# Cross-attention, second pass: eight key tiles of a block taken as 4 and 4 instead of 3, 3 and 2

## The reference

```python
def _L1_xattn_ref(x, latents, Wq, Wkv, Wout, gm, bm, gl, bl):
    ...
    xn = layernorm(x, gm, bm)            # x is the context, 8192 rows
    ln = layernorm(latents, gl, bl)      # 512 rows
    q = ln @ Wq
    kv_input = jnp.concatenate([xn, ln], axis=-2)
    kv = kv_input @ Wkv
    k, v = jnp.split(kv, 2, axis=-1)
    ...
    q, k, v = (heads(q), heads(k), heads(v))   # 8 heads of 64
    q = q / scale
    sim = jnp.einsum('bhid,bhjd->bhij', q, k)
    sim = sim - jax.lax.stop_gradient(jnp.max(sim, axis=-1, keepdims=True))
    attn = jax.nn.softmax(sim, axis=-1)
    out = jnp.einsum('bhij,bhjd->bhid', attn, v)
    ...
    return out @ Wout
```

## Time and profile before

| what | value |
|---|---|
| median of 3 runs | 2656.38 us (2655.33 to 2661.38) |
| the profiled execution | 2653.46 us |
| its span | 2651.8 us |
| mean granted TensorE clock | 0.969 |
| second pass of the cross-attention | about 1335 to 1864 us |
| TensorE busy | 2490.5 us, 94% |
| VectorE busy | 1809.0 us, 68% |
| ScalarE busy | 1122.2 us, 42% |

### The profile page before, as it was taken

How to read it: one execution, slowest core, us unless ns; L and a number is a source line. 1 busy time by engine, 2 the same in 40 slices (tenths; PEclk the granted TensorE clock), 3 DMA queues, 4 the chain that set the end, 5 groups by cost and what they waited for, 6 DMA issues and landing times.

```text
span 2651.8 us, 33253 instructions
## 1 busy us (share of the span) xinstructions
PE 2490.5 (94%) x11614; PEld 1681.0 (63%) x11618; DVE 1809.0 (68%) x1885; ACT 1122.2 (42%) x1366; POOL 592.2 (22%) x404
## 2 busy tenths in 40 slices
PE   6999989988776999999999999999898899999998
PEld 5778877654334777776655555555586777777775
DVE  5878855499988677778976666666445766666665
ACT  2334422466344222222255555555233455455543
POOL 4555544488842211111100000000000000000000
PEclk9999998999877999999999999999898899999999
DMA  7667755722021343343233232232112255666663
GB/s 276 231 237 259 264 153 171 258 72 72 2 101 42 127 169 148 127 182 136 96 124 108 96 96 73 96 108 84 64 64 115 104 219 214 237 229 230 216 218 137
DMA packets 124235, 394.70 MB, mean 149 GB/s; under 512 B 23728, under 2 KB 39292, under 8 KB 97136
## 3 DMA queue, kind: packets, MB, share of 16 engines
q1 hardware_dynamic: 95584, 326.82, 34.8%
q10 hardware_dynamic: 28560, 66.66, 7.2%
HBM read 304.14 MB, written 89.30 MB: 148 GB/s over the span
## 4 chain that ended last, share of the span: by engine, by line
PE 79%; DVE 8%; DMA 5%; POOL 3%; issue 3%; ACT 2%; ACTq 0%; SPq 0%; DVEq 0%; POOLq 0%
PE ps L2109 18%; PE ps L2110 17%; PE ps L2111 17%; PE ps L2496 10%; PE ps L2506 9%; PE ps L2403 3%; DMA w_halves<-unit_lo 3%; DVE ps L1642 2%; POOL work L951 1%; PE ps L2757 1%; DMA wT_lo<-w_halves 1%; DMA sh_raw<-in_s_parts 1%; DMA x_res<-in_x 1%; POOL work L932 1%; DVE ln_st L1512 1%
## 5 line engine op out<-in xcount | busy, mean ns | idle before, releaser
L1862 DVE TENSOR_TENSOR sums<-sums,pT 128x1024 f32<-128x1024 f32 x272 | 319.2, 1222 | 194.0 <-ACT pT L1341 192.9
L1800 DVE SCALAR_TENSOR_TENSOR peak<-ps,rs_all,peak 128x1024 f32<-128x1024 f32 x272 | 335.7, 1279 | 93.9 <-PE ps L2403 93.6
L1341 ACT ACTIVATE pT<-ps,rs_all 128x1024 f32<-128x1024 f32 x272 | 284.8, 1111 | 230.8 <-PE ps L2496 184.9
L2506 PE MATMUL ps<-pT,values 128*64 128x512 f32 x1088 | 256.4, 602 | 0.0
L2226 PE MATMUL ps<-work,ident 128*128 128x512 f32 x256 | 130.3, 641 | 33.6 <-POOL work L932 18.6
L1001 POOL TENSOR_TENSOR cT_lo<-cT_raw,cT_hi 128x512 fp32r<-128x512 f32 x60 | 77.6, 1293 | 352.1 <-ACT cT_hi L1290 352.1
L2506 PEld LDWEIGHTS ps<-pT,values 128*64 128x64 f32 x1088 | 68.8, 136 | 132.9 <-issue 112.0
L1996 DVE TENSOR_TENSOR rgu_lo<-rgu_raw,rgu_hi 128x2048 fp32r<-128x2048 f32 x64 | 143.9, 2289 | 5.1 <-ACT rgu_hi L1424 5.0
L894 POOL TENSOR_TENSOR ctx_lo<-ctx_raw,ctx_hi 128x512 fp32r<-128x512 f32 x64 | 105.2, 1643 | 131.7 <-DVE ctx_hi L1547 131.7
L1642 DVE TENSOR_TENSOR_SCAN ps<-ps,work 128x1024 f32<-128x1024 f32 x50 | 114.3, 2285 | 13.2 <-ACT ps L1213 11.2
L1028 POOL TENSOR_SCALAR ln_ve<-ln_mv 128x1 f32<-128x1 f32 x4 | 1.5, 379 | 537.0 <-DVE ln_mv L1513 537.0
(11 more groups left out here) (470 smaller groups left out, 6429.9 us busy)
## 6 DMA issues: line engine op xcount, KB each, us to landing
rgu_raw<-in_r_gate_up SPq DMA_DIRECT2D x64, 1024.0 KB, 4.8
rd_raw<-in_r_down SPq DMA_DIRECT2D x32, 1024.0 KB, 4.8
sh_raw<-in_s_parts SPq DMA_DIRECT2D x32, 768.0 KB, 4.3
key_rows<-key_hi SPq DMA_DIRECT2D x17, 1024.0 KB, 3.9
key_rows<-key_lo SPq DMA_DIRECT2D x17, 1024.0 KB, 6.0
value_rows<-values SPq DMA_DIRECT2D x17, 1024.0 KB, 8.9
ctxT_raw<-in_ctx_T SPq DMA_DIRECT2D x16, 1024.0 KB, 6.8
ctx_raw<-in_ctx SPq DMA_DIRECT2D x16, 1024.0 KB, 8.5
```

The source lines that it names most:

```text
L1341: nc.scalar.activation(pT[:, i], ps[:, b:b + 2], ACT.Exp, scale=rs_all[:, bass.ds(c * KT + attend_tile(j, i)[1], 1)]).then_inc(s4_exp.sem, 1)
L1800: nc.vector.scalar_tensor_tensor(peak[:, p], ps[:, b:b + 2], rs_all[:, bass.ds(c * KT + kt, 1)], peak[:, p], ALU.mult, ALU.max).then_inc(s ...
L1862: nc.vector.tensor_tensor(sums[:, p], sums[:, p], pT[:, i], ALU.add).then_inc(s4_sum.sem, 1)
L2506: done = nc.tensor.matmul(ps[e * DK:(e + 1) * DK, 6 + p], values[:, s, kt, h * DK:(h + 1) * DK], pT[:, i, e], start=start and kt == 0, sto ...
```

## The change

`attend_groups` gives blocks 2 to 32 two groups, (0, 1, 2, 3) and (4, 5, 6, 7). Blocks 0 and 1 keep four groups of two, and block 33 keeps 3, 3 and 2. The products behind a block's first group are now of tiles 4 to 7 of the block before, except in blocks 1 and 2, whose predecessors end with the group (6, 7). For that reason blocks 2 and 3 are written out on TensorE, and its first loop has 6 turns instead of 7. In block 2, now a plain number, tile 2 waits for the last shift rows and not for an exponential, since its place has not been used before. ScalarE, VectorE and SyncE have the same instructions and waits as before.

```diff
 def attend_groups(j):
 
-    return ((0, 1), (2, 3), (4, 5), (6, 7)) if isinstance(j, int) and j < 2 else ((0, 1, 2), (3, 4, 5), (6, 7))
+    if isinstance(j, int) and j < 2:
+        return ((0, 1), (2, 3), (4, 5), (6, 7))
+    if isinstance(j, int) and j == BLOCKS - 1:
+        return ((0, 1, 2), (3, 4, 5), (6, 7))
+    return ((0, 1, 2, 3), (4, 5, 6, 7))
...
                     else:
                         if isinstance(j, int) and j == 1:
                             shift_transpose(3)
-                        weigh_values(j - 1, 1 - s, 0 if isinstance(j, int) and j == KCHUNKS else half, (6, 7),
-                                     stop=isinstance(j, int) and j == KCHUNKS)
+                        weigh_values(j - 1, 1 - s, 0 if isinstance(j, int) and j == KCHUNKS else half,
+                                     (6, 7) if isinstance(j, int) and j <= 2 else (4, 5, 6, 7), stop=isinstance(j, int) and j == KCHUNKS)
 
             attend_pe(0, 1, 0, 32, start=True)
             attend_pe(1, 0, 0, 32)
-            with pe.Fori(0, LEFT) as q:
-                attend_pe(q * 2 + 2, 1, 0, q * 80 + 112)
-                attend_pe(q * 2 + 3, 0, 0, q * 80 + 112)
+            for j in range(2, 4):
+                attend_pe(j, 1 - j % 2, 0, 112)
+            with pe.Fori(0, LEFT - 1) as q:
+                attend_pe(q * 2 + 4, 1, 0, q * 80 + 192)
+                attend_pe(q * 2 + 5, 0, 0, q * 80 + 192)
```

## The result

The changed kernel takes 2646.95 us (median of 22 runs, 2637.16 to 2651.07), the kernel before 2654.94 in the runs beside it (22 runs, 2641.55 to 2661.38). The ratio is 0.997 with a 95% interval of 0.9961 to 0.998, so 5 to 10 us faster. The profiled execution has a span of 2643.0 us, against 2651.8.

The account below looks back on a forecast made before the run. TensorE's own order of work, busy 94%, was taken as the bound. With the load becoming the limit, 3.4 us from 28 blocks plus 0.7 from three gave 4.1, taken as 4.5: 2656.38 to 2651.9 us, range 2645.5 to 2663.

Parts of the forecast that it names:

- (a): TensorE, blocks 2 to 32: one round trip fewer each, 0.35 us, 10.9 us in all if nothing new waits.
- (b): Fourth tile of a group waits for the first tile's exponential, twice a block; 0 to 0.06 us each, 0.06 taken.
- (c): Next block's load is issued later, at 7.77 us, and becomes the limit: period 15.17 instead of 15.29 us.
- The sign that I had named: Period from one block's first similarities to the next in the changed profile: 15.1 to 15.2 us, not 14.9.
- Full gain (1): Loads land in time and exponentials hold nothing up; 7.1 to 10.9 us gained, 2645.5 to 2649.3 us; chance 0.18.
- The load wait with a loss (2): TensorE waits on `kv_loaded` at the heads of 28 blocks; 5.7 to 25 us slower, 2662 to 2682; chance 0.16.
- Exponentials (3): Fourth tile held 0.25 us instead of 0.06 by its exponential; 4.7 us slower, 2661 us; chance 0.09.
- The loop part (d): Blocks 2 and 3 written out on TensorE, and block 2's other wait for tile 2: no effect.

Follow-up runs that it names:

- keys early: Changed kernel with a block's keys and scale rows issued after the similarities, only values still after the products; 2641.02 us, ratio 0.9949 to before.
- groups of two: Kernel before with groups of two tiles in all blocks, four round trips instead of three; 2666.93 us, ratio 1.0063 to before.
- groups of six: Changed kernel with keys early and groups (0, 1) and (2 to 7); ratio 0.9974 to before, pass 483.08 us.
- The second comparison: The changed kernel run again unaltered, against the kernel before; 2649.7 us, ratio 0.9979.
- the two kernels with the latest loads: Changed kernel with the load held back until tile 4's similarities, ratio 1.0104; changed kernel with scale rows issued ahead of keys and values, ratio 1.0067.

## Why the prediction was right

**The round trip** (a). Predicted 0.35 us each, 31 of them, 10.9 us. Measured with nothing in the way (keys early against before): 489.41 - 478.08 = 11.3 us, 0.37 each; from the other side, groups of two, 0.37 in the mean of all blocks but 17. Right, shown twice. What in a round trip costs the time was not separated. The rows only show where it stands: 0.32 instead of 0.23 us from the last pair of a similarity group to the products, 0.34 instead of 0.23 behind the first pair of a group, and 0.14 behind the products. That the change of the tiles' shape does it, and not for instance the order of the weight loads, is argued and not shown.

**The fourth tile** (b). Predicted up to 0.06 us for each wait. In the changed kernel the exponential, the weight load and the matmul of the fourth tile, and the addition that takes the same result, answer to the earlier trace rows:

```profile
1501.49 4.13 ACT L1345 ACTIVATE pT<-ps,rs_all 128x1024 f32<-128x1024 f32 x4 [3.43 <-PE ps L2500]
...
1502.54 0.42 PE L2500 MATMUL ps<-shift_rows,scale_rows 64*128 64x512 f32 x2
1502.66 0.19 PEld L2500 LDWEIGHTS ps<-q_lo,key_hi 64*128 64x128 f32 x2
1502.73 4.63 DVE L1866 TENSOR_TENSOR sums<-sums,pT 128x1024 f32<-128x1024 f32 x4 [2.93 <-ACT pT L1345]
```

The weight load stands at 1502.66, 0.12 behind the matmul it would have gone with (1502.54), 2.74 us after the group's start, inside the 2.68 to 2.81 that were read from the exponential. Its matmul started at 1502.77, 0.23 after the one before, so unhindered. The wait is real and costs 0, since half of the weight load's lead of 0.23 us took it up. I had taken the upper end, a release at 2.81 and 0.11 from the weight load to the matmul. The weight load came at 2.74, and the groups of six show a matmul 0.03 behind its weight load, so the 0.11 is no least distance either.

**The load** (c). The mechanism is the one predicted: issue, landing, and a block that starts with the later of the two. This is the step that carried the forecast, and its size was somewhat off. Predicted were an issue at 7.77, 6.9 to the last byte, 0.45 to the count and 0.05 to go on: 15.17 us. Measured: 7.71 and 7.32, which is 15.03. So 0.06 too much is from (b), 0.08 from the landing. The saving of a usual block was thus 0.26 to 0.28 us and not 0.12. What made the total less wrong than that were the seven longer blocks, which I had not predicted: they hold the mean at 15.11. The sign that I had named, a period of 15.1 to 15.2 us, fits this mean and not the usual block, and that is luck. Over the pass: 4.5 us predicted, 6.25 and 3.7 measured in two traces.

**The total.** 2651.9 us was predicted against a median of 2656.38; with the runs beside it the median of before is 2654.94 and the change is worth 8.0 us (5.3 to 10.4), which is more than the 4.5 predicted. The second comparison gave 0.9979, 5.6 us. Both are more than the passes of the two traces show, 6.25 and 3.7, but both intervals take these in, so chance may be all of it. What moves the stages outside the pass stays open: two traces of the same changed kernel already differ by 1.3 us at the start of block 2 and by 1.9 behind the pass.

**The rivals.** Full gain (1) needed the loads to land in time; they do not, but with keys early it is what one gets. The load wait with a loss (2) was the right wait at a price that did not come about: its point was put at 7.47 us from issue to landing, and it is 7.3; only single blocks passed it, as block 19 with 16.08 us. The rule of the Trainium skill that the prediction names (DMA: Bandwidth & Descriptors, Anatomy of one DMA), by which most of 2 us lies between the last byte and the semaphore, is stated there for transfers issued by GpSimd; these are issued by SyncE. It is not borne out here: from last bytes at 1514.50 to TensorE's start at 1514.95 is 0.45 us. Exponentials (3) cost nothing at four and five tiles, and 0.16 us a block at six. The loop part (d) cost nothing.

## What to carry to other kernels

When TensorE is busy throughout and no wait is to be seen, count how often it changes from one kind of matmul to the other: here each round trip cost 0.37 us, and the price is in the starts of the instructions, not in any idle time. Then ask what a longer group pushes back: here the release of a buffer moved from 5.1 to 7.7 us into a block, and half of the gain (5.1 of 11.3 us, in a second trace 7.7) went to a load that had looked well hidden. Release each part of a buffer with its own last reader (keys with the similarities, values with the products), and the cover is back.

## What the runs showed of the hardware

- From the first issue to the start of the waiting engine, 1.5 MB in three transfers from DRAM took 7.30 to 7.38 us in the median of each of the five traces in which TensorE waited for them (132 of 145 loads 7.16 to 7.70, the longest 8.73), whether small transfers followed or not. In the load shown above 0.45 of it lay behind the last byte. Two 6 KB transfers ahead of the large ones delayed the end by 0.8 us, the time of their issue; behind them they were free.
- Loads that meet an instruction fetch are mostly longer. The load issued at 1416.45 in the changed kernel was waited for until 1424.44, 7.99 us, and in the 8.5 us around it (1416 to 1424.5) there was one packet of the instruction queue:

```profile
1416.45 0.35 SPq L784 DMA_DIRECT2D key_hi<-key_rows  x1
...
q8 instruction: 1, 0.02, 0.7%
...
1424.44 0.50 PE L2500 MATMUL ps<-q_lo,key_hi 64*128 64x512 f32 x2 [0.75 <-DMA scale_rows<-sd_rows_dram]
```

  The longest of this trace, 8.35 us behind an issue at 1627.84, has one too. Over the same five traces 14 of the 145 loads have such a packet: eleven took 7.97 to 8.73 us, three 7.27 to 7.35. Of the 131 without, one took 8.13 and the others at most 7.80. So the two go together; that the fetch is the cause was not tested by itself.
- A weight load may come late by about half of its lead of 0.23 us and cost nothing: with a lead of 0.11 left (1502.66 to 1502.77) nothing was late, with 0.07 and 0.03 the pair of matmuls behind came 0.04 and 0.07 us late.
- Within the pass the granted clock fell from 1.00 to 0.50 after three waits, of 2.52, 2.13 and 1.94 us, in the two kernels with the latest loads, for some 3 us each time, and cost about 1.5 us beyond the wait. In the changed kernel itself the longest waits were 1.07 and 1.27 us in the two traces, and it stayed at 1.00.
